# Adding the causal mask with a matmul, and taking one minimum per PSUM bank, in a fused attention, FFN and scan kernel

## The reference

```
x = x + attention(layernorm(x))      # 16 heads, latent q and kv, rotary part, causal
x = x + ffn(layernorm(x))            # weights looked up in a table of 16 values
x = x + ssm(layernorm(x))            # input projection, gated scan over time, output projection
x = x + ffn(layernorm(x))
```

```
scores = einsum('bqhd,bkhd->bhqk', q, k) * scale
scores = where(causal, scores, -inf)
probs  = softmax(scores, axis=-1)
out    = einsum('bhqk,bkhd->bqhd', probs, v)
```

## Time and profile before

| | |
|---|---|
| three timed runs | 942.59, 935.8 and 941.74 us, median 941.74 |
| the profiled execution | 935.25 us; its span from first to last instruction 933.4 us |
| mean granted clock | 0.949 |
| TensorE busy (matmuls) | 786.5 us, 84% of the span |
| VectorE busy | 753.4 us, 81% |
| ScalarE busy | 586.6 us, 63% |
| GpSimd busy | 510.1 us, 55% |

### The profile page before, as it was taken

How to read it: one execution, slowest core, us unless ns; L and a number is a source line. 1 busy time by engine, 2 the same in 40 slices (tenths; PEclk the granted TensorE clock), 3 DMA queues, 4 the chain that set the end, 5 groups by cost and what they waited for, 6 DMA issues and landing times.

```text
span 933.4 us, 17579 instructions
## 1 busy us (share of the span) xinstructions
PE 786.5 (84%) x4556; PEld 669.5 (72%) x4556; DVE 753.4 (81%) x2388; ACT 586.6 (63%) x1386; POOL 510.1 (55%) x545
## 2 busy tenths in 40 slices
PE   4768888988778998777899889997999957679998
PEld 4657767777667777666787778876888845568887
DVE  3768999999699998879999999985656669855555
ACT  3457767877576887766888788874333355633332
POOL 2599999999999999999999998100000000000000
PEclk9778999999888999899999999998999998979999
DMA  9600000000000000000000100000000000000000
GB/s 260 199 1 0 2 1 1 1 2 1 5 1 1 1 2 1 4 2 1 1 2 2 35 1 1 1 1 1 1 0 0 0 0 1 0 1 23 22 22 22
DMA packets 15393, 14.66 MB, mean 16 GB/s; under 512 B 5792, under 2 KB 14432, under 8 KB 15040
## 3 DMA queue, kind: packets, MB, share of 16 engines
q1 hardware_dynamic: 13792, 11.41, 4.2%
q0 software_dynamic: 624, 2.12, 0.7%
q10 hardware_dynamic: 880, 0.04, 0.1%
HBM read 11.46 MB, written 2.10 MB: 15 GB/s over the span
## 4 chain that ended last, share of the span: by engine, by line
PE 45%; DVE 27%; issue 21%; ACT 4%; DVEq 2%; DMA 1%; ACTq 0%; SPq 0%
PE bank L529 9%; PE bank L531 9%; PE bank L530 9%; PE bank L1270 4%; DVE pt_lo L981 3%; DVE bias_m L934 2%; DVE q_tok L951 2%; DVE prob L972 2%; DVE o_b L987 2%; PE bank L1284 2%; PE bank L1287 2%; DVE qt_lo L958 1%; DVE q_rot L949 1%; PE bank L506 1%; PE bank L1297 1%
## 5 line engine op out<-in xcount | busy, mean ns | idle before, releaser
L646 POOL TENSOR_SCALAR hot<-idx_gu,lut 128x256 f32<-128x256 bf16 x165 | 195.1, 1182 | 16.7
L696 ACT ACTIVATE prob<-bank,bias_m 128x128 f32<-128x128 f32 (+3 forms) x256 | 135.3, 528 | 81.5 <-DVE bias_m L934 80.5
L934 DVE CUSTOM_DVE_ANT_0 bank<-bank,mask 128x128 f32<-128x128 f32 (+3 forms) x256 | 125.9, 492 | 14.5 <-issue 13.6
L651 POOL TENSOR_TENSOR w_gu<-w_gu,hot 128x256 f32<-128x256 f32 x165 | 122.7, 744 | 13.8
L1270 PE MATMUL bank<-ident,prob 128*128 128x128 f32 x640 | 101.9, 283 | 29.6 <-issue 17.1
L981 DVE TENSOR_TENSOR pt_lo<-bank,pt_hi 128x512 fp32r<-128x512 f32 x160 | 108.8, 680 | 4.3 <-ACT pt_hi L724 4.2
L1270 PEld LDWEIGHTS bank<-ident,prob 128*128 128x128 f32 x640 | 75.0, 144 | 47.7 <-issue 24.0
L529 PE MATMUL bank<-kt_hi,qt_hi 128*128 128x128 f32 (+3 forms) x256 | 91.6, 358 | 14.9 <-ACT prob L696 6.0
L646 POOL TENSOR_SCALAR hot<-idx_dn,lut 128x256 f32<-128x256 bf16 (+1 forms) x90 | 98.0, 1089 | 9.1
L724 ACT CAST pt_hi<-bank 128x512 fp32r<-128x512 f32 x160 | 93.3, 583 | 14.8 <-PE bank L1287 7.9
L1284 PE MATMUL bank<-pt_hi,v_hl 128*128 128x512 f32 x160 | 71.7, 448 | 19.0 <-issue 7.5
(11 more groups left out here) (194 smaller groups left out, 2266.8 us busy)
## 6 DMA issues: line engine op xcount, KB each, us to landing
x<-in_L_attn_a_x_dram SPq DMA_DIRECT2D x4, 512.0 KB, 7.5
wo_nat<-in_L_attn_a_wo_dram SPq DMA_DIRECT2D x1, 2048.0 KB, 12.4
out_dram<-x SPq DMA_DIRECT2D x16, 128.0 KB, 1.7
wqu<-in_L_attn_a_wq_up_dram SPq DMA_DIRECT2D x2, 768.0 KB, 7.5
wqr<-in_L_attn_a_wq_rope_dram SPq DMA_DIRECT2D x4, 192.0 KB, 7.5
raw_dn<-in_L_ffn_down_idx_dram POOLq DMA_DIRECT2D x1, 688.0 KB, 10.8
raw_gu<-in_L_ffn_gate_idx_dram POOLq DMA_DIRECT2D x1, 640.0 KB, 7.6
raw_gu<-in_L_ffn_up_idx_dram POOLq DMA_DIRECT2D x1, 640.0 KB, 8.4
```

The costliest lines, as they stand in the source:

```text
L646: nc.gpsimd.tensor_scalar(dst, idx[:, c:c + n], float(v), lut[:, v:v + 1], ALU.is_equal, ALU.mult).then_inc(lut_hot, 1)
L651: nc.gpsimd.tensor_tensor(w, w, hot[:, 0:n], ALU.add).then_inc(lut_sum, 1)
L696: nc.scalar.activation(prob[:, n % 2, h, 0:w], bank[2 + h % 2][:, 0:w], ACT.Exp, bias=bias_m[:, n % 2, h:h + 1], scale=-1.0, accum_out=den ...
L934: nc.vector.tensor_tensor_reduce(out=bank[2 + h % 2][:, 0:w], in0=bank[2 + h % 2][:, 0:w], in1=mask[:, TB * P - w:TB * P], scale=1.0, scal ...
```

## The change

TensorE adds the mask. The mask shrinks to its last 128 columns; ScalarE makes float32r copies of it and of the identity matrix once. Behind the three matmuls of a head's scores comes a fourth, `ident_r` times `mask_r`, into the last 128 columns of that head's scores. This is done for all 256 head and query tile pairs.

Scores of several heads share a bank: `heads_per(n)` is 4 in tile 0 (4 x 128 columns fill a bank), 2 in tile 1, 1 in tiles 2 and 3. `scores` is then called once for each group, issues all its heads back to back, and raises its semaphore once, behind the last. `row_max` is a plain tensor_reduce with minimum over the group's heads, 4, 2 or 1 results at once; it neither writes the bank nor needs the memset and the accumulator read. `exp` stays one call for each head and waits for the group's minimum. A group's place in the order is that of its first head, so in tile 0 all scores come at the place of `scores(s-2, 0)`.

The waits that count groups, and those that protect banks 2 and 3 against the down projection, are rewritten to fit.

```diff
+def heads_per(n):
+
+    return max(1, G // 2 ** tile_of(n))
...
-        mask = keep("mask", [P, TB * P], F32)
+        mask = keep("mask", [P, P], F32)
+        mask_r = keep("mask_r", [P, P], F32R)
+        ident_r = keep("ident_r", [P, P], F32R)
...
+        def score_bank(n, h):
+
+            w, k = (tile_of(n) + 1) * P, h // heads_per(n)
+            return bank[2 + (groups_before(n) + k) % 2], h % heads_per(n) * w, w
...
             def exp(b, n, h):
-                w = (tile_of(n) + 1) * P
-                act.wait_ge(s_max, b * HEADS * TB + G * n + h + 1)
+                o, c0, w = score_bank(n, h)
+                act.wait_ge(s_max, b * GROUPS + groups_before(n) + h // heads_per(n) + 1)
...
-                settle(n % 2 * G + h)
-                nc.vector.tensor_tensor_reduce(out=bank[2 + h % 2][:, 0:w], in0=bank[2 + h % 2][:, 0:w],
-                                               in1=mask[:, TB * P - w:TB * P], scale=1.0, scalar=3e38,
-                                               op0=ALU.add, op1=ALU.min,
-                                               accum_out=bias_m[:, n % 2, h:h + 1]).then_inc(s_max, 1)
+                hp = heads_per(n)
+                if h % hp:
+                    return
+                o, _, w = score_bank(n, h)
+                dve.wait_ge(s_mm, b * GROUPS + groups_before(n) + h // hp + 1)
+                free_after(dve, s_exp, 1 + b * HEADS * TB + G * (n - 2) + h + hp)
+                nc.vector.tensor_reduce(out=bias_m[:, n % 2, h:h + hp],
+                                        in_=o[:, 0:hp * w].rearrange("p (h k) -> p h k", h=hp),
+                                        axis=mybir.AxisListType.X, op=ALU.min).then_inc(s_max, 1)
...
-                free_after(pe, s_exp, 1 + b * HEADS * TB + G * n + h - 1)
-                split_mm(bank[2 + h % 2][:, 0:w],
-                         [(qt_hi[:, n % 2, h, :], qt_lo[:, n % 2, h, :], kt_hi[:, 0:w], kt_lo[:, 0:w])],
-                         True, True).then_inc(s_mm, 1)
+                free_after(pe, s_exp, 1 + b * HEADS * TB + heads_through(k - 2))
+                for j in range(hp):
+                    c0, c1 = j * w, (j + 1) * w
+                    split_mm(o[:, c0:c1],
+                             [(qt_hi[:, n % 2, h + j, :], qt_lo[:, n % 2, h + j, :], kt_hi[:, 0:w], kt_lo[:, 0:w])],
+                             True, False)
+                    last = nc.tensor.matmul(o[:, c1 - P:c1], ident_r[:, :], mask_r[:, :], start=False, stop=True)
+                last.then_inc(s_mm, 1)
```

More of the change, by code:

```diff
@@ L46, in blocks_before, with groups_before, heads_through @@
     return sum(tile_of(m) + 1 for m in range(n))
+def heads_per(n):
+    return max(1, G // 2 ** tile_of(n))
+def groups_before(n):
+    if n < 0:
+        return groups_before(UNITS + n) - groups_before(UNITS)
+    return sum(G // heads_per(m) for m in range(n))
+GROUPS = groups_before(UNITS)
+def heads_through(k):
+    if k < 0:
+        return k + 1
+    ends = [G * n + h for n in range(UNITS) for h in range(heads_per(n), G + 1, heads_per(n))]
+    return ends[k]
 def step_of(b, nb, step, n, *k):
@@ L583, in _ @@
             sp_.dma_start(sin2[:, :, :], c_sin).then_inc(tables_in, 16)
-            sp_.dma_start(mask[:, :], c_mask).then_inc(tables_in, 16)
+            sp_.dma_start(mask[:, :], c_mask[:, (TB - 1) * P:TB * P]).then_inc(tables_in, 16)
             sp_.dma_start(wo_nat[:, :, :], wo.rearrange("(c p) d -> p c d", p=P)).then_inc(wo_in, 16)
@@ L669, in _ @@
             nc.scalar.copy(warm[:, :], one[:, :])
+            act.wait_ge(ident_in, 16)
+            nc.scalar.copy(ident_r[:, :], ident[:, :]).then_inc(mask_ready, 1)
             def down_copy(b, t):
@@ L691, in exp @@
             def exp(b, n, h):
[L692 to L693 removed]
+                o, c0, w = score_bank(n, h)
+                act.wait_ge(s_max, b * GROUPS + groups_before(n) + h // heads_per(n) + 1)
                 if h == 0:
                     free_after(act, pt_mm, b * BLOCKS + blocks_before(n - 1))
[L696 removed]
+                nc.scalar.activation(prob[:, n % 2, h, 0:w], o[:, c0:c0 + w], ACT.Exp,
                                      bias=bias_m[:, n % 2, h:h + 1], scale=-1.0,
@@ L776, in _ @@
             nc.scalar.activation(a_neg[:, :], a_neg[:, :], ACT.Exp).then_inc(a_exp, 1)
+            act.wait_ge(tables_in, 16 * 3)
+            nc.scalar.copy(mask_r[:, :], mask[:, :]).then_inc(mask_ready, 1)
             for s in range(LEAD):
@@ L1248, in scores @@
             def scores(b, n, h):
-                w = (tile_of(n) + 1) * P
+                hp = heads_per(n)
+                if h % hp:
+                    return
+                o, _, w = score_bank(n, h)
+                k = groups_before(n) + h // hp
                 if h == 0:
@@ L1308, in pe_slot @@
                 do(p_transpose, s - 5, 3)
-                if nb is not None and s in (9, 10):
-                    pe.wait_ge(sq, 2 * nb * TB + 4 * (s - 8))
                 do(scores, s - 3, 1)
@@ L1319, in pe_slot @@
                 do(values, s - 5, 2)
+                if nb is not None and s in (9, 10):
+                    pe.wait_ge(sq, 2 * nb * TB + 4 * (s - 8))
                 do(scores, s - 3, 2)
@@ L1370, in _ @@
                     pe.wait_ge(prep_dve, S0)
+                if s == 2:
+                    pe.wait_ge(mask_ready, 2)
                 pe_slot(s, 0, None)
```

10 lines of the change are left out of this document (4 added, 6 removed).

## The result

| | before | changed |
|---|---|---|
| median of ten runs | 940.38 us | 931.19 us |
| range | 934.47 to 943.21 | 926.36 to 934.69 |
| profiled execution, span | 935.25, 933.4 | 933.49, 931.7 |
| mean granted clock, profiled | 0.949 | 0.956 |

The ratio is 0.9908, 95% interval 0.9883 to 0.9934: the change makes the kernel 0.9% faster. I had forecast 946 us, a loss of 7.6 us. The time lies in the range of 925 to 961, but the change went the other way. The two profiled executions are 1.8 us apart, where the medians are 9.2 apart: that of before lies at the low end of its ten, that of the change at the high end of its own. So I read from the traces where waits and clock levels are, and sizes of the whole from the medians.

What follows compares the result with a forecast made beforehand. VectorE was taken as full and TensorE nearly so in tiles 2 and 3, with waits in narrow tiles. Terms 4.2 + 2.4 - 0.6 + 3.5 + 2 - 2.6 - 1.3 = 7.6 us gave 942.9, plus 3.6: 946 us, range 925 to 961.

Steps and rivals of the forecast that it cites:

- The jump back: Loop's jump back: VectorE's 3.55 us wait for head 1 goes, `rope_q` moves up; 1.3 us saved each, twice -2.6.
- VectorE's 4.51 us: Rival, VectorE's wait at its jump: waits for code may go or come, 9 us either way, 937 to 955; chance 0.13.
- First unit of a batch: Tile 0, first unit: no spare on TensorE's path, so longer first scores cost +1.4 us, three times, 4.2.
- Second unit: Second unit of a batch: path growth 1.17 less spare 0.4, +0.8 us, three times, 2.4.
- the 2 for the first batch: First batch, at a lower clock with start-up waits between: +2 us, an estimate.
- The other units of tile 1: Other three units of tile 1: growth 1.06 less spare 0.53, +0.5 us, nine times 4.5, less 1: 3.5.
- tile 2, -1.3: Tile 2: spare exceeds the mask's 0.33 us, so VectorE's saving is earned, 16 x -0.08 = -1.3 us.
- tile 3, 0: Tile 3: saving of -1.3 us cancelled by +1.4 from units with less than 0.41 us to spare.
- the rival wanted 0.45 in every one: Rival, tiles 2 and 3: TensorE becomes the bound, mask paid in full, 32 x 0.45 = 14.4 us, 962; chance 0.17.
- VectorE, the minimum and its readout: VectorE: plain pass priced as the fused, 0.61 us over 512 columns; memsets and readouts 0, except 0.08 a slot before `out_low`.
- ScalarE is not what the round waits for: ScalarE: `exp` of heads 1 to 3 waits less in narrow tiles, but this was counted as 0.
- The matmuls of a group pack closer: Rival, score groups in tiles 0 and 1: matmuls 0.06 us each in place of 0.11; 4 us less, 935; chance 0.04.

Runs made afterwards that it cites:

- e7: The kernel before with the loop over the batches of attention written out on all three engines: 920.67 us, ratio 0.9814 to before.
- e8: The changed kernel with the loop over the batches written out on all three engines: 922.77 us, ratio 0.983 to before.
- e1: The changed kernel with one head to a group in every tile, mask by matmul and plain minimum kept: 931.02 us, ratio 0.9912 to before.
- e5: The changed kernel with 512 scratch memsets on VectorE, two for each head around its group's minimum: 929.29 us, ratio 0.9909 to before.
- e13: The changed kernel with 64 memsets of scratch columns at VectorE's start: ratio 0.9928 to before.
- e11: The kernel before with 64 memsets of scratch columns at VectorE's start: ratio 0.9984 to before.
- e14: The kernel before with 8 memsets of scratch columns at VectorE's start: ratio 0.997 to before.
- e16: The changed kernel with groups of two in tile 1 alone, one head elsewhere, and the batch loop written out: ratio 0.9813 to before.
- e15: The changed kernel with one head to a group everywhere and the batch loop written out: 916.5 us, ratio 0.9761 to before.
- e17: The kernel before with the mask's matmul added (fused minimum kept) and the batch loop written out: ratio 0.9862 to before.
- e18: e15 without the mask's matmuls, so the causal mask is left out and something else is computed: ratio 0.9753 to before.
- e3: The changed kernel with groups of four in tile 0 alone, one head to a group elsewhere: 934.16 us, ratio 0.9954 to before.
- e6: The kernel before with the mask's matmul added behind each head's three, nothing else changed: 945.65 us, ratio 1.0074 to before.
- e2: The changed kernel with groups of two in tile 1 alone, one head to a group elsewhere: 929.75 us, ratio 0.9879 to before.
- e4: The changed kernel with groups of two in tiles 0 and 1, one head elsewhere: 927.48 us, ratio 0.9868 to before.

## Why the prediction was wrong

**The step that failed is "The jump back: ... Worth 1.3 each, the four instructions of `rope_q`; twice -2.6".** Its mechanism was right as far as it went: VectorE's wait for head 1 goes from 3.55 to 0.22, `rope_q` moves up, and the next to be late is `qt_low`, by 0.76. Its size was not right. The jumps give 10 us (17 less 7, from e7 and e8; 6 to either side), four times the term. By the table the groups, of which alone the term speaks, bring about 7 of them (e1 to the change, 0.015 to 0.008) and the plain minimum with VectorE's code in another place the rest (0.019 to 0.015). I had priced the work that VectorE moves into the gap. Three things were missing:

- TensorE's own wait shortens, 3.41 to 2.09, in the kernels with groups in tile 1. The last semaphore wait in front of the jump was head 0's, for `exp` of the head two before, and TensorE stood at it (0.38 us, at 237.83). Afterwards come three matmuls and the jump. With the group that wait names an `exp` done long before, and eight matmuls lie between the last matmul of `project` and the jump. From the end of the last releaser to the first matmul behind the jump it is about 4.1 us before (237.77 to 241.85) and 4.4 in the change (`o_b`'s copy ends at 244.75, matmul at 249.13), so the jump costs the same, and more work lies over it. The packet of code shows it too: the one on queue 8 starts at 239.22 before, 0.78 behind the last matmul's end, and at 246.07 in the change, 0.96 ahead of it, and the matmuls go on 1.67 and 1.81 us after it has landed. Queue 8 over TensorE's wait before (238.45:241.85), and over its last matmuls in the change (246.00:247.03):

```profile
q8 instruction: 1, 0.02, 1.8%
```

```profile
q8 instruction: 1, 0.02, 7.6%
```

  At all ten jumps of the kernels with groups in tile 1 the packet starts 0.6 to 1.2 us ahead of the wait, at all 16 of the others with the loop 0.2 to 0.9 us into it, and from its landing to the first matmul it is 1.6 to 1.9 us in all 26. No run moved that semaphore wait alone: that it is what holds the jump back is argued from the traces.
- The clock. I read 0.93 in the earlier trace rows and did not ask where it was lost. Two falls to 0.50 a jump make the matmuls behind it take 0.63 for 0.39, as the third `q_up` row of before shows. What one fall costs, as an estimate: e5 and e13 are the change with memsets added and have one at the first jump; their two slots take 19.6 and 19.1 us where the change's take 18.2. So of the 7.7 us that the profiles show at a jump about 1 is luck of that execution; the second fall, behind VectorE's long wait, may be as much, which no run shows by itself.
- VectorE's 4.51 us. I had it as a rival with a chance of 0.13, nine microseconds either way. It went to 2.33, and e11 and e14 price it at 1 to 3 us.

**First unit of a batch, +1.4 each.** The profile shows 3.4, 1.5 and 2.1 (10.8, 10.3, 10.3 before; 14.2, 11.8, 12.4 after). The largest is the one in which the clock falls inside the group of sixteen, which I had not priced. Where it holds, the sixteen take 1.84 us (354.01 to 355.85), the 1.8 that I had forecast; where it falls, 2.75. Behind the start of a batch's first scores, by 0.7 to 2.2 us, the clock falls in 14 of the 21 cases in kernels with groups in tile 0, and in 5 of the 39 in kernels without. Second unit, +0.8 each: 0.7, 0.7 and 0.5 in the profile. By the medians groups of four cost 3 to 4 us in all with the loop and 2 without (e16 to e8), against my 4.2 + 2.4 + part of the 2 for the first batch: too high by half or more.

**The other units of tile 1, +3.5; tile 2, -1.3; tile 3, 0.** Four wide slots of the second batch took 7.77, 8.32, 10.38 and 9.66 before and take 7.78, 8.37, 10.39 and 9.66 after; in the first and third batch two slots of four are longer, by 0.1 to 0.24, where the rival wanted 0.45 in every one. TensorE does not become the bound, though it is busy 48.28 of 50 us. That rival is out, and with it the whole of my upper end. The +3.5 of tile 1 can be read only without jumps: e15 to e16 has it, 2.7, 0.9 and 1.1 us in three batches' tile 1 slots, but between e7 and e8 these slots change by -0.8, +0.7 and 0.0: the plain minimum takes 1.4, 0.4 and 0.9 off them (e17 to e15). Tile 2's four slots are 2.8 and 1.3 us shorter from e7 to e8, where I had 0.3 (in the first of them e7's clock falls). Each of these is read from one execution.

**VectorE, the minimum and its readout.** Distance to the next instruction: 0.60 for the plain pass of 512 against 0.61, as I said. What I left out is the latency. The minimum is read by `exp`, which starts 0.51 behind the fused pass and 0.45 behind the plain one. First before, then e1, VectorE and ScalarE:

```profile
236.70 0.42 DVE L934 CUSTOM_DVE_ANT_0 bank<-bank,mask 128x256 f32<-128x256 f32 x1
237.21 0.47 ACT L696 ACTIVATE prob<-bank,bias_m 128x256 f32<-128x256 f32 x1 [0.72 <-DVE bias_m L934]
```

```profile
239.00 0.41 DVE L971 TENSOR_REDUCE bias_m<-bank 128x1 f32<-128x256 f32 x1
239.45 0.48 ACT L729 ACTIVATE prob<-bank,bias_m 128x256 f32<-128x256 f32 x1 [0.32 <-DVE bias_m L971]
```

Over 111 such waits of `exp` in e7, 104 in e17 and 94 in e15 the sum goes from 78.7 to 73.1 to 66.3 us; but in all ScalarE is idle for 125 of the 570 us from 60 to 630, in e7 and in e15 alike. I had said that ScalarE is not what the round waits for, and that the readout is worth 0 but for 0.08 a slot. Outside the jumps the plain pass earns 0.6% to 1.0%, 6 to 9 us: e7 to e18, which has no mask matmul, and e17 to e15. My 0.08 a slot is 5 us over all 64. That the latency is the reason is an inference; the gain is measured.

**The sum.** Without its jump term my forecast is 7.6 + 2.6 = 10.2 us slower; e7 and e8 say 1.5 us slower, within noise of nothing. With the loop the jumps bring 10 where I had 2.6. Both errors point the same way, 7.5 and 8.7, and together they make 16 of the 17 us between +7.6 and -9.2. Step by step without jumps: the matmul +4.5 (e7 to e17), the plain minimum -9.5 (to e15), groups in tile 1 +4.9 (to e16), groups of four in tile 0 +1.6 (to e8), each to about 5 us. So a second step failed, **what the plain minimum saves**: its price on VectorE was right, 0.60 against 0.61, but for the rest of it I allowed only 0.08 a slot and nothing for `exp`, and the measured 9.5 us are about twice the 5 that this gives over all slots. The groups in tile 1 cost what I had said, as far as 5 us can tell.

**A slip in a rival.** In "The matmuls of a group pack closer" the growth in tile 1 comes to 0.9 by its own terms (twice 0.84 less 0.36, less 0.36, plus 0.26), not 0.7, which makes that rival about 1 us slower. It was out all the same: at full clock the matmuls of the group are 0.11 apart (209.22 to 209.33 in the changed kernel).

## What to carry to other kernels

A jump back costs what the engines behind it lose, not only the wait that the profile puts there: look at the granted clock in the slots that follow, at what last released the waiting engine in front of the jump, and at the transfers of instructions around it. Write a loop of three passes out and time it, before a gain inside it is believed: here that was worth twice the change, and left nothing of the change's gain. When an instruction's result is waited for, compare the start of its reader, not only the start of its neighbour on its own engine.

## What was not expected of the hardware

- Eight memsets at the start of VectorE's program, in a gap where it waits for x, change its wait for code at a jump 240 us later from 4.5 to 2.2 us, in the same loop of the same work: one packet of code of 8 KB lies in it in place of two.
- TensorE's clock fell to 0.50 behind the waits of 3 us and more that I looked at (before, e1, e3, e6, e11, e14). Behind waits of 1.8 to 2.3 us at the same place it held at both jumps of the change, at one of two in e2 and e4, and at none in e5 and e13. It also fell to 0.50 inside the group of sixteen matmuls, behind a wait of 1.59 us and 0.8 us of 128-column matmuls. Behind the same wait and three or four such matmuls it held in the kernel before, and in all but 5 of 39 cases over the kernels without groups in tile 0.
